# Placing the steps of a recurrence between the dense slots of a memory layer: by a table instead of every second slot

## The reference

```python
def _L1_cond_ref(x, h0, Wx, Wh, b):
    xW = jnp.einsum('ntd,dk->ntk', x, Wx) + b
    def step(carry, xw_t):
        prev_h, prev_c = carry
        a = xw_t + prev_h @ Wh
        i, f, o = sigmoid(a[:, :H]), sigmoid(a[:, H:2*H]), sigmoid(a[:, 2*H:3*H])
        g = jnp.tanh(a[:, 3*H:])
        next_c = f * prev_c + i * g
        next_h = o * jnp.tanh(next_c)
        return ((next_h, next_c), next_h)
    _, hs = jax.lax.scan(step, (h0, c0), xW_t)

x = x + _L0_ffn_ref(_L0_cond_ref(x, ...), ...)    # experts, then a memory layer (top-8 of 4096 keys)
x = x + _L1_ffn_ref(_L1_cond_ref(x, ...), ...)    # this recurrence, then attention and experts
```

## Time and profile before

| | |
|---|---|
| time, median of 3 runs | 2982.59 us (2981.89 to 2984.08) |
| span of the profiled execution | 2977.3 us; no other time is listed for it |
| TensorE busy | 2840.2 us, 95% of the span |
| VectorE, ScalarE, GpSimd busy | 64%, 41%, 17% |
| mean granted TensorE clock | 0.985 |
| first and last recurrent step | 493.6 and 1970.1 us |

### The profile page before, as it was taken

One profiled execution on the slowest core, in us unless ns is written; L12 is line 12 of the kernel. 1 busy time (PEld: TensorE's weight loads), 2 busy tenths in 40 slices (PEclk: granted clock), 3 DMA queues, 4 the chain that ended last, 5 costly groups with the idle time before them and its releaser, 6 DMA issues.

```text
span 2977.3 us, 72660 instructions
## 1 busy us (share of the span) xinstructions
PE 2840.2 (95%) x28558; PEld 2187.9 (73%) x28558; DVE 1919.1 (64%) x6577; ACT 1215.2 (41%) x2721; POOL 491.4 (17%) x616
## 2 busy tenths in 40 slices
PE   8999979999999999999999999978999859999998
PEld 4895467777777777777777777645676639999998
DVE  4553587777777777777777777466777654444443
ACT  2332232333334343434343333235555525555554
POOL 0555400000000000000000000012334313333333
PEclk9999989999999999999999999999999979999999
DMA  3552300101010000101010101111222232222222
GB/s 141 175 158 82 140 2 23 33 23 34 23 34 30 26 32 25 36 24 34 23 34 23 33 23 33 37 36 41 70 77 63 59 121 33 37 37 40 37 37 33
DMA packets 94322, 148.90 MB, mean 50 GB/s; under 512 B 20048, under 2 KB 76240, under 8 KB 90896
## 3 DMA queue, kind: packets, MB, share of 16 engines
q1 hardware_dynamic: 73728, 107.83, 11.0%
q0 software_dynamic: 20112, 36.40, 6.0%
q10 hardware_dynamic: 144, 0.03, 0.0%
HBM read 95.93 MB, written 48.27 MB: 48 GB/s over the span
## 4 chain that ended last, share of the span: by engine, by line
PE 87%; DVE 6%; DMA 2%; ACT 2%; issue 2%; SPq 0%; POOL 0%; POOLq 0%; DVEq 0%; ACTq 0%
PE ps L1008 16%; PE ps L827 15%; PE ps L2075 9%; PE ps L1077 8%; PE ps L2090 8%; PE ps L1044 4%; PE ps L989 4%; PE ps L420 2%; PE ps L431 2%; PE ps L857 2%; PE ps L858 2%; PE ps L1560 2%; PE ps L1516 1%; PE ps L266 1%; PE ps L267 1%
## 5 line engine op out<-in xcount | busy, mean ns | idle before, releaser
L827 PEld LDWEIGHTS ps<-arena 128*128 128x128 f32 x4096 | 536.4, 192 | 29.1 <-issue 2.9
L1008 PE MATMUL ps<-arena 128*128 128x256 f32 x2048 | 550.7, 392 | 3.0 <-DVE arena L998 2.0
L827 PE MATMUL ps<-arena 128*128 128x128 f32 x4096 | 538.9, 276 | 0.9 <-ACT arena L835 0.9
L1008 PEld LDWEIGHTS ps<-arena 128*128 128x128 f32 x2048 | 354.7, 190 | 164.1 <-issue 132.9
L835 ACT ACTIVATE arena<-ps 128x256 f32<-128x256 f32 x512 | 196.0, 383 | 546.4 <-PE ps L827 545.9
L1077 PE MATMUL ps<-arena 128*16 128x256 f32 x4096 | 270.6, 382 | 8.4 <-DVE arena L1107 7.6
L2075 PE MATMUL ps<-arena 128*128 128x128 f32 x2272 | 265.4, 275 | 0.1
L1803 POOL MEMSET arena<- 128x3072 f32 x1 | 2.7, 2658 | 1569.6 <-PE ps L1008 1569.6
L2075 PEld LDWEIGHTS ps<-arena 128*128 128x128 f32 x2272 | 259.4, 192 | 0.4 <-issue 0.3
L2090 PE MATMUL ps<-arena 128*128 128x256 f32 x1136 | 256.8, 379 | 0.0
L1098 DVE SCALAR_TENSOR_TENSOR arena<-arena 128x128 f32<-128x128 f32 x256 | 73.7, 288 | 280.6 <-ACT arena L1089 280.6
(11 more groups left out here) (287 smaller groups left out, 4631.3 us busy)
## 6 DMA issues: line engine op xcount, KB each, us to landing
xw_scratch<-arena SPq DMA_DIRECT2D x32, 512.0 KB, 2.7
arena<-xw_scratch SPq DMA_DIRECT2D x256, 64.0 KB, 2.7
arena<-in_W SPq DMA_DIRECT2D x16, 1024.0 KB, 5.2
ys_scratch<-arena SPq DMA_DIRECT2D x71, 128.0 KB, 1.8
xn_scratch<-arena SPq DMA_DIRECT2D x32, 129.0 KB, 3.0
arena<-in_xT SPq DMA_DIRECT2D x8, 512.0 KB, 8.1
arena<-in_kinT SPq DMA_DIRECT2D x8, 512.0 KB
arena<-in_xtb SPq DMA_DIRECT2D x32, 128.0 KB, 2.2
```

The costliest lines, as they stand in the source:

```text
L827: m = e.matmul(bank(b)[:, 128 * i:128 * i + 128], kin[:, k, 2 * jp + i, :], xcT[:, k, 128 * blk:128 * blk + 128], start=(k == 0), stop=(k ...
L1008: m = e.matmul(bank(7)[:, 0:256], G[blk % 2][:, j, :], kout[:, j, :], start=(j == 0), stop=(j == 31))
```

## The change

Steps get their position from a table, step_pos. It is computed in tenths of a slot: a step comes 1.6 slots (GAP10) behind the one before it, not before ready (16 b + 26 for block b), and a block's last step not before one slot behind the next block's second XW. Positions are rounded up. Steps whose position lies in the last pass or before it stand in the loop (IN of them), and the others behind it (TAIL). Seeds stand at most two slots ahead of their step. ScalarE's and VectorE's lists now go by slots too. VectorE's place2 and the second half of place move by a slot. norms_of is shifted with TAIL. Names DB, SB and ND allow for blocks that are computed in another way. SPARSE_AT is empty, so ND is 32, DB[b] is b, and every wait that they stand in has its old value.

```diff
+        SPARSE_AT = ()
+        NSP, ND = len(SPARSE_AT), 32 - len(SPARSE_AT)
+        SB = [c + k for k, c in enumerate(SPARSE_AT)]
+        DB = [b for b in range(NBLK) if b not in SB]
...
-        LAG = 13
-
-        def step_of(i, k):
-            t = 8 * i - LAG + k
-            return range(t, t + 1) if 0 <= t < 8 * NBLK else ()
-
-        def seed_of(i, k):
-            t = 8 * i - LAG + 1 + k
-            return range(t, t + 1) if 0 <= t < 8 * NBLK else ()
+        GAP10 = 16
+        END = 16 * ND
+
+        def ready(b):
+            return 16 * SPARSE_AT[SB.index(b)] + 17 if b in SB else 16 * DB.index(b) + 26
+
+        def input_product(b):
+            return 16 * SPARSE_AT[SB.index(b)] + 12 if b in SB else 16 * DB.index(b) + 20
+
+        step_pos, turn10 = [], 0
+        for t in range(8 * NBLK):
+            turn10 = max(turn10 + GAP10, 10 * ready(t // 8))
+            if t % 8 == 7 and t // 8 + 1 < NBLK:
+                turn10 = max(turn10, 10 * input_product(t // 8 + 1) + 10)
+            step_pos.append(-(-turn10 // 10))
+        IN = len([p for p in step_pos if p < END])
+        TAIL = 8 * NBLK - IN
+        step_pos = step_pos[:IN] + [END + 2 * k for k in range(TAIL)]
+        seed_pos = [step_pos[0] - 2] + [max(step_pos[t - 1], step_pos[t] - 2) for t in range(1, 8 * NBLK)]
+        steps_at = {g: [t for t in range(8 * NBLK) if step_pos[t] == g] for g in range(-32, END + 2 * TAIL)}
+        seeds_at = {g: [t for t in range(8 * NBLK) if seed_pos[t] == g] for g in range(-32, END + 2 * TAIL)}
...
         def norms_of(k):
+            k += 13 - TAIL
             return range(max(0, 2 * k - 4), max(0, 2 * k - 2)) if k < 7 else range(k + 3, k + 4)
...
                 for jp in range(16):
-                    if jp % 2 == 0:
-                        for t in step_of(i, jp // 2):
-                            step_tensor(e, t)
+                    for t in steps_at[16 * i + jp]:
+                        step_tensor(e, t)
                     if i >= 0:
                         outmm_tensor(e, i, jp)
```

More of the change, by code:

```diff
@@ L1027, in x1_tensor, with x1_free_vector @@
[L1027 to L1036, removed]
+        def x1_free_vector(e, b):
+            bb = b % 2
+            e.wait_ge(s[f"xr{bb}"], 16 * (b // 2 + 1))
+            if b >= 2:
+                e.wait_ge(s[f"x1s{bb}"], 16 * (b // 2))
+                e.wait_ge(s["x1tr"], b - 1)
@@ new lines, in x1_tensor, with x1_scalar @@
+        def x1_tensor(e, d):
+            b = DB[d]
+            e.wait_ge(s["x1"], b + 1)
+            if d + 3 < ND:
+                e.wait_ge(s["tk"], 20 * (d + 3) + 3)
+            e.transpose(bank(1)[:, 0:128], x1[:, b % 2, 0:128], ident)
+            e.transpose(bank(1)[:, 128:256], x1[:, b % 2, 128:256], ident).then_inc(s["x1tr"], 1)
+        def x1_scalar(e, d):
+            b = DB[d]
+            e.wait_ge(s["x1tr"], b + 1)
+            e.activation(xcT[:, :, 128 * b:128 * b + 128], bank(1)[:, 0:256].rearrange("p (a b) -> p a b", a=2),
@@ L1212, in peer_scalar @@
                             ztrans_scalar(e, 0)
-            for k in range(LAG):
-                for t in step_of(NBLK, k):
-                    gates_scalar(e, t)
-                for t in seed_of(NBLK, k):
-                    seed_scalar(e, t)
-                for t in step_of(NBLK, k):
-                    cell_scalar(e, t)
+            for k in range(TAIL):
+                t = IN + k
+                gates_scalar(e, t)
+                if t + 1 < 8 * NBLK:
+                    seed_scalar(e, t + 1)
+                cell_scalar(e, t)
                 if k == 0:
-                    x1_scalar(e, NBLK - 1)
+                    x1_scalar(e, ND - 1)
                 for n in norms_of(k):
@@ L1273, in peer_vector @@
-                    if more and k == 7:
+                    if more and jp == 0:
+                        best2_vector(e, i + 2, 4, 8)
+                    if more and jp == 1:
+                        place2_vector(e, i + 2)
+                    if more and jp == 5:
+                        rows_vector(e, i + 2)
+                    if more and jp == 7:
+                        ztrans_vector(e, i + 2)
+                    if next_ and jp == 8:
+                        best_vector(e, i + 3, 0, 8)
@@ L1274, in peer_vector @@
+                    if next_ and jp == 9:
+                        best_vector(e, i + 3, 8, 16)
+                    if next_ and jp == 11:
+                        place_vector(e, i + 3, 2, 4)
+                    if next_ and jp == 12:
+                        place_vector(e, i + 3, 6, 11)
+                    if next_ and jp == 13:
+                        place_vector(e, i + 3, 11, 16)
+                    if more and jp == 15:
                         onehot_vector(e, i + 2, 0)
-            for k in range(LAG):
-                for t in step_of(NBLK, k):
-                    cell_vector(e, t)
-                    hidden_vector(e, t)
+            for k in range(TAIL):
+                cell_vector(e, IN + k)
+                hidden_vector(e, IN + k)
@@ L1279, in peer_vector @@
                 if k == 1:
[L1280 removed]
+                    xw_vector(e, ND - 1)
                 for n in norms_of(k):
```

154 lines of the change are left out of this document (59 added, 95 removed).

## The result

The changed kernel takes 3011.36 us (median of 4 runs, 3010.79 to 3012.85). The kernel before, run beside it, takes 2982.24 us (2980.67 to 2984.08). The ratio is 1.0100, 95% interval 1.0085 to 1.0114, or 29.1 us. Forecast were 22.7 us and 3005.3. The direction and both causes were right, and the sum was 6.4 us short: 3011.36 lies 0.6 us inside the upper end of the forecast's own range, 2998 to 3012.

The account below looks back on a forecast made before the run. TensorE, full in the dense stretch, and the step chain behind it were taken as bounds. Dense holds of 16.1 us plus 6.6 at the end gave 22.7, added to 2982.59: 3005.3 us, own range 2998 to 3012, overall 2990 to 3020.

Parts of the forecast that it names:

- both causes: TensorE holds at slot 15 in the dense passes, 16.1 us, and a later end behind them, 6.6 us.
- The hold at slot 15: Dense passes 1 to 28: TensorE waits 0.57 us for the step at slot 15, 28 x 0.57 = 16.0 us.
- No other hold: Dense passes: TensorE waits for no step or product except at slot 15; no added time elsewhere.
- The 0.22 us of room at slot 2: Dense passes, step at jp 2: needs 3.99 us after the step before and has 4.21, so no hold.
- rival (d): VectorE falls behind after slot 15, step at jp 2 holds TensorE 0.5 us a pass: 3019 us; chance 15%.
- Rival (b): Dense stretch hides slack of some 0.6 us a pass or more, so only the end costs: 2989 us; chance 10%.
- Rival (c): Dense passes: slack plus hidden holds of the old spacing let each pass gain, say, 0.5 us: 2975 us; chance 5%.
- The lists by slots cost nothing: ScalarE's list moved from pairs of slots to slots: same operations and table loads, covered by idle, costed at nothing.
- The rule on weight loads: Skill's rule: a wait at S could hide a 0.19 us load of the following O, 5 us less; not used.
- The end: Passes 30, 31 and behind: emptied slots delay x1 and the last seed, saved step becomes a wait; 6.6 us later.
- Step 232: Pass 30: seed there at 21.3 to 22.6 us after the pass's first O, step at 22.2.
- "All behind unchanged": Steps 248 to 255, the norms beside them and everything behind take the same time as before.

Follow-up runs that it names:

- the pair of kernels: The changed kernel (3011.36 us) and the same with VectorE's pairs_vector moved behind the hidden vector in slot 14 (2999.67 us).
- gap20: Changed kernel with GAP10 = 20, so steps are two slots apart again while the lists stay by slots: 2982.17 us, ratio 1.000 to the kernel before.
- dense_only: Changed kernel with the 1.6-slot spacing only for steps below 224, two slots apart from there on: 2998.78 us, ratio 1.0061 to the kernel before.
- the dose test: Changed kernel with more VectorE work (place_vector for the last five keys) between cell and hidden vector of slot 14: 3042.19 us.
- warm: Changed kernel with filler matmuls in slots 7 to 9 of pass 30 and behind step 247: 3015.68 us, ratio 1.0104 to the kernel before.
- early2: Changed kernel with steps two slots apart, all two slots earlier, first seeds one slot ahead of their step: 2997.48 us, ratio 1.0050 to the kernel before.
- after_again: The changed kernel run once more, unaltered, beside other kernels on one chip: 3008.73 us, ratio 1.0092 to the kernel before.
- after: The changed kernel itself in its first measurement: median 3011.36 us, profiled execution 3011.06 us.
- end_only: Changed kernel with steps two slots apart below step 224 and the 1.6-slot spacing from there on: 2995.13 us, ratio 1.0045 to the kernel before.
- pairs_late: Changed kernel with VectorE's pairs_vector moved behind the hidden vector in slot 14: 2999.67 us, ratio 1.0061 to the kernel before.
- place_between: Changed kernel with the last five keys' place_vector moved from slot 13 to slot 14, ahead of pairs_vector: 3042.19 us.
- no_trip: Changed kernel whose seeds of steps 248 to 255 read the previous block's buffer without waiting for a load: 3011.67 us, ratio 1.0087 to the kernel before.
- no_trips_end: Changed kernel whose seeds from step 232 on read block 28's buffer, loads of blocks 29 to 31 left out: 3004.29 us, ratio 1.0079 to the kernel before.

## Why the forecast was right, and where it was short

**The hold at slot 15** was forecast at 0.57 a pass, of which 0.46 from pairs_vector. Measured were 3.53 us from S to S (3.51), or 0.59 a pass, and in the pair of kernels 0.46 for pairs_vector. From step 0 to step 224 the changed kernel takes 1377.30 us and gap20 1360.91, which is 16.4 for 28 holds (forecast 16.0). Up to the first O of pass 30 only 15.76 are seen because step 0 stood 0.9 earlier in that execution, by scatter in the stage before. As dense_only the part cost 16.9.

**No other hold**: right. The listed waits are 28 and all at slot 15. The 0.22 us of room at slot 2 was enough, so rival (d) fell. Rival (b) fell with the 28 waits and the dose test, since a hold is paid in full. Rival (c) wanted hidden holds of the old spacing to be won back; a pass grew from 48.73 to 49.31 us, that is by 0.58, all of its hold, so nothing was won back.

**The lists by slots cost nothing**: right, by gap20.

**The rule on weight loads.** The S that was held starts at 1246.24 and O behind it at 1247.22, the same 0.98 as behind an S that waits for nothing. The engine's weight loads of that S, of that O and of the D behind it:

```profile
1246.21 0.59 PEld L1089 LDWEIGHTS ps<-arena 128*16 128x16 f32 x16 [0.68 <-issue]
1247.22 0.73 PEld L1012 LDWEIGHTS ps<-arena 128*128 128x128 f32 x4 [0.42 <-issue]
1247.98 1.08 PEld L831 LDWEIGHTS ps<-arena 128*128 128x128 f32 x8
```

The O's loads begin with the O, not during the wait. D's loads do begin ahead, 0.21 before its matmuls at 1248.19. What the Trainium skill says in "TensorE: Matmul & The Clock Gate", section on the 16 sub-arrays, that loads are pulled ahead of matmuls, the trace shows at D, but not at the O behind S, with a wait or without, and the 5 us that it would have taken off were not taken off.

**The end.** The mechanism was right: emptied slots, x1 late, the last seed late, the saved step turned into a wait. Two terms were mis-sized or missing.
- Step 232 was forecast 22.2 after the first O of pass 30, with the seed at 21.3 to 22.6. The seed came at 23.2 and the step at 23.7, since the trip through memory took 8.76 us (8.72 and 8.80 in warm and early2). I had taken 6.75 from the trip for step 248, which took 7.16 now. The trace of before has the trip for step 232 itself, at 7.66, and I didn't read it:

```profile
1883.44 0.32 SPq L1058 DMA_DIRECT2D xw_scratch<-arena  x1
...
1891.10 0.39 ACT L1085 ACTIVATE ps<-arena 128x256 f32<-128x256 f32 x1 [2.70 <-DMA arena<-xw_scratch]
```

  Now the store was issued at 1900.70 and the loads behind its landing at 1905.24, 4.5 us later, where the last block had 2.9 and this block 3.3 before: the difference is in the landing of the store. Why it lands later there stays open.
- The clock. The sum had no term for it. With the matmuls of pass 30 at 3.68 instead of 1.99, step 233 was 2.95 behind the forecast, and 2.0 remained when x1 of block 31 was added (67.4 instead of 65.4). From there the forecast's distances held to 0.3: step 244 +2.0, seed and step 248 +2.3. So the end became 8.8 longer instead of 6.5 (6.6 with the 0.1 ahead of it). The smaller part of this is the clock's: in after_again the matmuls behind step 232 kept it, step 233 was 1.2 behind the forecast, and the end was 85.9, still 1.7 over the forecast's 84.2.

**"All behind unchanged"** was the larger miss. The attention stage took 372.4, which is 3 us more than in gap20 (369.3) and 5 more than in the profiled execution before (367.3), at a lower clock in its first stretches. Where the end has late seeds it is slow in seven executions: 372.0 to 372.4 in after, after_again, end_only, pairs_late and place_between, 373.6 in no_trip, 373.8 in warm. It takes 369.3 in gap20 and dense_only, and 369.6 in no_trips_end. That suggests the waits for memory as the cause, but early2 speaks against it. Its seeds waited 6.01, 1.90 and 3.47 us and its step 232 ran at the lower clock, and still its attention stage took 369.8. The window 33 us behind its step 255:

```profile
2016.60:2046.60 30.00, 22.19 (x188) 0.94 0.01 2
```

So late seeds at the end are not enough for the slow start, and its cause stays open. What the forecast had wrong is the term for all behind step 248, which it put at nothing without a row for it.

Against gap20's execution it adds up: 15.7 up to pass 30, 9.0 more at step 248 and no more at the first row-max product, 3.1 in the attention stage and 1.5 in what follows, together the 29.3 us by which the spans differ. The 1.5 are within the scatter: what follows the stage took 620.8 us in this execution and 618.5 in after_again's.

No version was found that beats the kernel before. One edit was not tried: ScalarE's list has the seed ahead of the tanh of the cell, so the late seed of 248 also holds the tanh of step 247. Behind the seed S came 1.24 us later, and 0.44 in step 232, where nothing else was waiting; the difference of 0.8 is below what the medians can tell.

## What to carry to other kernels

Where a dependent chain runs beside an engine that is full, the distance between two links must be covered by other work of that engine, and everything that another engine's queue does between the links belongs to the chain. An uneven table costs at its tightest pair in every pass, while its loose places give nothing back. A link that is saved behind the dense work is only a gain if the input of the links behind it comes earlier as well. And where a tuned engine gets an idle stretch that it didn't have, a clock fall in the work that follows belongs in the range: here it cost 1 to 3 us at a place, in some executions and not in others. A wait for memory is read at its own place in the trace, and not at another block's.

## What the hardware showed that was not expected

- Idle between short groups of matmuls can be followed by the 1.2 GHz level: after idle of 1.64 and 1.49 us 8 matmuls of O took 3.68 instead of 1.99, after 1.89 and 1.27 half an input product took 3.78 instead of 1.98, and after 3.37 an S took 1.91 instead of 1.06. With the same idle it didn't fall in another execution of the same kernel (1.99 behind 1.63 and 1.30 in after_again). The rows show that it happens, not from what point on.
- The same trip through memory, from the issue of the store to the first seed, took 6.75 us for the last block and 7.66 for block 29 before, and 7.16 and 8.76 after; 8.72 and 8.80 are block 29's in warm and early2.
- MATCH_VALUE_LOAD and FIND_INDEX8 are listed with some 0.07 and 0.22 us, but a pair follows a pair every 0.20 to 0.22.
